# The order of a fused attention and graph-attention kernel laid out anew: five hand-written lists and a table of PSUM banks

## The chip, the cores and the metric

The kernel runs on one core of a Trainium2 chip. The metric is the device time of one execution in microseconds (us); lower is better. Five instruction streams work side by side: TensorE (PE, matrix products, with weight loads shown apart as PEld), ScalarE (ACT), VectorE (DVE), GpSimd (POOL) and SyncE (SP), which here only issues DMAs. They meet through semaphores alone.

## The reference, cut to what matters

Eight batches of 1024 nodes with 128 features pass two layers over the same 1024x1024 adjacency matrix `adj`. Each layer begins with a layer normalisation and a ReLU and ends with a residual sum.

```
h   = relu(layernorm(x))
# layer 0: attention with 4 heads of 32, softmax taken within each of 8 chunks of 128 keys
s   = clip(q @ k.T / sqrt(32), -10, 10);  s = where(adj == 0, -10, s)
ctx = sum over the chunks of softmax(s of the chunk) @ v of the chunk
x   = x + layernorm(ctx @ Wo.T + bo + h) * gamma + beta
h   = relu(layernorm(x))
# layer 1: graph attention over a full row
Wh  = h @ W
e   = leaky_relu(Wh@a1 [i] + Wh@a2 [j], 0.2), -inf where adj has no edge
x   = x + elu(softmax(e) @ Wh)
```

## The kernel before, in words

All constants (masks and transposed weights) are made once at the start; after that every batch `b` goes through the same operations, and the operations of several batches overlap.

Layer 0 of a batch: `stats_x`, `moments_x`, `rstd_x` and `apply_x` normalise a half of 512 nodes; `turn_x` transposes it; `query`, `key` and `value` are its projections. SP copies the projections into head-separated stacks with DMAs (`stack_query`, `stack_key`, four DMAs each). Then come 32 groups of two heads: `scores` (PE) into one of two PSUM slots, `exp` (ACT), `probs` (DVE, which clips and masks), and for every step of two groups `sums` and `context` (PE), `log_sum` and `inverse` (ACT), `gather` (DVE multiplies, POOL adds). `project`, `residual`, `stats_y`, `rstd_y`, `apply_y`, `gamma`, `beta` and `x1` end the layer. `load_residual` is SP's DMA that brings h and x back for this.

Layer 1 of a batch: `rstd_z`, `apply_z`, `turn_hidden`, `wh`, then `peaks` (DVE, eight row maxima with the mask), `row_shift` (POOL), `near_row` and `base_row` (PE), sixteen times `leaky` (DVE), `hide` (mask added, on POOL or DVE) and `gat_exp` (ACT), then `share` (PE, eight of them), `invert`, `below`, `above`, `exp_below`, `add_x1`, `add_below` and `store_out`.

What runs when is written out by hand. There is one table for each engine: `TENSOR`, `SCALAR`, `VECTOR`, `GPSIMD` and `SYNC`. For every batch and name a table gives one place for each index `k`. `in_order(engine)` adds `b * PLACES` (9600) to the place and sorts; each engine then issues its operations in exactly that order, and each operation carries its own semaphore waits. An engine that stands at a wait does nothing of what is listed behind it. A place is only a sort key: a number in it costs nothing by itself.

The string `BANKS` says which of four PSUM banks each operation with a result in `work` uses, in the order of TensorE's list. An operation waits until the user of that bank before it has been read (`free_bank`).

Waits that the prediction touches:

```
dve.wait_ge(x_loaded[k], (b + 1) * 16)                  # stats_x
dve.wait_ge(rest_loaded, 16 * 6)                        # bias_row on DVE
sp.wait_ge(h_stored[k], b * 16)                         # load_x: store_h of the batch before has landed
sp.wait_ge(h_stored[k], (b + 1) * 16)                   # load_residual
act.wait_ge((keys_stacked if before[0] else queries_stacked)[before[1]], (before[2] + 1) * 64)   # query, key
pool.wait_ge(res_loaded[k], 32 * (b + 1))               # residual, beta
act.wait_ge(see_made, 2 * k - 1)                        # cast (ACT)
```

`rest_loaded` counts the six small loads (W, two of a, bo, gamma, beta) that SP issues behind the eight 512 KB loads of `adj`. `parts` holds one half of a projection until its stack DMAs have read it, so `query` and `key` on ACT wait for stacks. `edges` on DVE makes the masks of one row tile; the first `probs` needs four of them.

Of the kernel before, what the change touches and what calls it, by code (L numbers as in the profile page):

```python
# [52 lines left out]
        "weights": [1817, 2924],  # L53
        "value": [1829, 2012],
        "scores": [2254, 2300, 2571, 2745, 2879, 3124, 3420, 3617, 3781, 4002, 4175, 4427, 4560, 4782, 4946, 5197,
            5361, 5526, 5778, 5911, 6075, 6248, 6381, 6633, 6721, 6975, 7314, 7447, 7699, 7778, 8030, 8120],
        "bias_row": [2498],
        "sums": [2957, 3179, 3836, 4230, 4614, 5089, 5252, 5670, 5966, 6524, 6776, 7030, 7502, 7833, 8181, 8659],
        "context": [3267, 3672, 4057, 4318, 4837, 5001, 5416, 5581, 6130, 6436, 6864, 7118, 7590, 7922, 8275, 8822],
        "project": [6293, 10229],  # L60
        "turn_hidden": [11515, 13038],
        "to_row": [11870, 13239],
        "wh": [13845, 14952, 15066],
        "base_row": [17051, 17141],
        "near_row": [17349, 19413],
        "share": [19632, 19850, 20319, 20536, 23047, 23219, 23437, 23773],
    },
    1: {
        "turn_x": [-6225, -4877],
        "query": [-5128, -1171],  # L70
        "key": [-3776, -2374],
        "value": [-2241, -1084],
        "scores": [-1217, -996, -833, -669, -505, -337, -174, -10, 154, 451, 584, 779, 1030, 1171, 1423, 1497,
            1862, 1960, 2224, 2357, 2528, 2704, 3084, 3130, 3392, 3506, 3726, 3830, 4081, 4433, 4479, 4818],
        "sums": [-614, -282, 45, 342, 834, 1226, 1552, 2103, 2412, 2759, 3185, 3884, 4136, 4622, 5036, 5243],
        "context": [-450, -119, 254, 922, 1314, 1640, 1753, 2015, 2596, 2976, 3274, 3973, 4324, 4534, 4873, 5664],
        "project": [2868, 9680],
        "turn_hidden": [8121, 12296],
        "to_row": [12163, 12745],
        "wh": [14729, 14961, 15120],  # L80
        "base_row": [15684, 16561],
# [1702 lines left out]
```

## Time and profile before

| what | value |
|---|---|
| time, median of 3 runs | 720.74 us (719.3 to 720.92) |
| profiled execution, time | 718.64 us |
| profiled execution, span of the trace | 716.9 us |
| DVE busy | 662.4 us (92%) |
| PE busy | 651.6 us (91%) |
| ACT busy | 651.6 us (91%) |
| POOL busy | 526.8 us (73%) |
| DMA | 68.53 MB |

The span is what lies between the first and the last instruction of the trace; the device time of the same execution is 1.7 us longer. The busy share is an average over a start, a long middle and an end that look different.

### The profile page before, as it was taken

The page shows a single profiled execution, that of the slowest core. Times are in us where ns is not written, and L with a number is a line of the kernel's source. Part 1 is how long each engine was busy: PE and PEld are TensorE (multiplying, and loading weights), DVE is VectorE, ACT ScalarE, POOL GpSimd, SP SyncE. Part 2 cuts the span into 40 slices and gives each one's busy share as a digit, 9 for nine tenths or more (in the row PEclk, how much of TensorE's full clock was granted, in tenths as well). Part 3 has the DMA queues.
Part 4 walks back from the last instruction along what each step waited for, and adds up shares of the span by engine and source line. Part 5 has one row for each costly group of instructions (what it writes and reads, how often), then busy time and mean ns, then how long its engine had stood idle before and what let it go on. Part 6 is the DMA issues. An engine that isn't in the chain of part 4 may idle for free.

```text
span 716.9 us, 13598 instructions
## 1 busy us (share of the span) xinstructions
PE 651.6 (91%) x4393; PEld 348.5 (49%) x4393; DVE 662.4 (92%) x1165; ACT 651.6 (91%) x1140; POOL 526.8 (73%) x629
## 2 busy tenths in 40 slices
PE   4389999999899999998999999999999999994976
PEld 2333333344345563546436464557336463564865
DVE  3599999999999999998999999999999999989976
ACT  6399999998999999998999999999999999987655
POOL 2324648656589877978789578998778779998864
PEclk9799999999999999999999999999999999998888
DMA  8742132324121225233222234222222312010111
GB/s 282 236 157 103 60 118 104 103 89 161 63 84 46 93 71 176 75 104 111 80 77 81 90 104 152 91 77 71 83 96 78 114 53 96 23 53 16 51 52 46
DMA packets 58647, 68.53 MB, mean 96 GB/s; under 512 B 5328, under 2 KB 35024, under 8 KB 58576
## 3 DMA queue, kind: packets, MB, share of 16 engines
q1 hardware_dynamic: 57568, 67.39, 27.9%
q8 instruction: 36, 0.59, 0.3%
q10 hardware_dynamic: 1008, 0.26, 0.2%
q14 instruction: 35, 0.29, 0.1%
HBM read 21.50 MB, written 12.58 MB: 48 GB/s over the span
## 4 chain that ended last, share of the span: by engine, by line
PE 39%; ACT 18%; DVE 17%; POOL 10%; issue 10%; DMA 5%; SPq 3%; DVEq 0%; ACTq 0%; POOLq 0%
PE work L1726 11%; PE score L1643 9%; DVE probs L1451 8%; PE work L1660 7%; PE work L1654 6%; ACT score L1296 6%; POOL ring L1248 3%; ACT ring L1364 3%; DVE ring L1542 2%; ACT inverse L1303 2%; ACT inverse L1306 2%; DVE scaled L1477 2%; DVE near_row L1521 2%; SPq L1098 1%; PE work L1618 1%
## 5 line engine op out<-in xcount | busy, mean ns | idle before, releaser
L1451 DVE SCALAR_TENSOR_TENSOR probs<-score,cap 128x1024 f32<-128x1024 f32 x256 | 307.9, 1214 | 11.6 <-ACT score L1296 9.0
L1296 ACT ACTIVATE score<-score 128x1024 f32<-128x1024 f32 x256 | 259.1, 1022 | 6.7 <-PE score L1643 5.2
L1643 PE MATMUL score<-query_stack,key_stack 128*128 128x512 f32 x512 | 188.3, 452 | 14.1 <-DVE probs L1451 10.3
L1223 POOL TENSOR_TENSOR gathered<-gathered,scaled 128x512 f32<-128x512 f32 x112 | 150.3, 1342 | 44.2 <-DVE scaled L1477 41.7
L1248 POOL TENSOR_TENSOR ring<-ring,see_t 128x512 f32<-128x512 f32 x112 | 134.5, 1211 | 22.4 <-DVE ring L1542 21.9
L1643 PEld LDWEIGHTS score<-query_stack,key_stack 128*128 128x128 f32 x512 | 78.6, 189 | 135.8 <-DVE probs L1451 104.7
L1660 PE MATMUL work<-probs,ones 128*32 128x512 f32 x1024 | 135.3, 604 | 1.0 <-DVE scaled L1477 0.4
L1654 PE MATMUL work<-probs,value 128*32 128x512 f32 x1024 | 133.6, 600 | 0.2
L1726 PE MATMUL work<-wh,ring 128*128 128x130 f32 x896 | 110.6, 279 | 12.8 <-ACT ring L1364 11.9
L1726 PEld LDWEIGHTS work<-wh,ring 128*128 128x128 f32 x896 | 107.1, 194 | 23.9 <-issue 16.1
L1364 ACT ACTIVATE ring<-ring,wh 128x512 f32<-128x512 f32 x128 | 90.0, 729 | 9.7 <-POOL ring L1248 7.7
L1306 ACT ACTIVATE inverse<-inverse 128x512 f32<-128x512 f32 x128 | 81.2, 639 | 0.4
L1477 DVE TENSOR_TENSOR scaled<-work,inverse 128x512 f32<-128x512 f32 x112 | 75.7, 680 | 4.8 <-ACT inverse L1306 3.9
L1303 ACT ACTIVATE inverse<-work 128x512 f32<-128x512 f32 x128 | 76.8, 603 | 2.2 <-PE work L1660 1.2
L1542 DVE SCALAR_TENSOR_TENSOR ring<-work,wh,to_row 128x512 f32<-128x512 f32 x96 | 69.6, 739 | 0.0
L1521 DVE CUSTOM_DVE_ANT_0 near_row<-to_row,see 128x1024 f32<-128x1024 f32 x48 | 67.1, 1397 | 0.7 <-ACT to_row L1342 0.3
L1654 PEld LDWEIGHTS work<-probs,value 128*32 128x32 f32 x1024 | 24.9, 108 | 60.9 <-issue 41.3
L1178 POOL TENSOR_TENSOR small<-small,eps 128x4 f32<-128x4 f32 x48 | 14.6, 304 | 54.1 <-DVE small L1430 53.8
L1660 PEld LDWEIGHTS work<-probs,ones 128*32 128x32 f32 x1024 | 24.7, 108 | 57.6 <-issue 43.3
L1181 POOL TENSOR_TENSOR small<-small,minus_half 128x4 f32<-128x4 f32 x48 | 49.6, 1034 | 3.8
L1253 POOL TENSOR_TENSOR gat_out<-gat_out,gat_x 128x256 f32<-128x256 f32 x30 | 25.0, 835 | 12.0 <-ACT gat_out L1382 12.0
L1670 PE MATMUL work<-h_t,w_t 128*128 128x512 f32 x64 | 33.4, 606 | 0.5 <-issue 0.2
(117 smaller groups left out, 844.5 us busy)
## 6 DMA issues: line engine op xcount, KB each, us to landing
query_stack<-parts SPq DMA_DIRECT2D x64, 256.0 KB, 2.6
key_stack<-parts SPq DMA_DIRECT2D x56, 256.0 KB, 2.5
x_in<-in_x SPq DMA_DIRECT2D x16, 256.0 KB, 3.2
h_kept<-x_in SPq DMA_DIRECT2D x16, 256.0 KB, 2.6
res<-h_kept SPq DMA_DIRECT2D x16, 256.0 KB, 2.9
h<-in_x SPq DMA_DIRECT2D x16, 256.0 KB, 3.4
x_kept<-res SPq DMA_DIRECT2D x16, 256.0 KB, 2.2
gat_x<-x_kept SPq DMA_DIRECT2D x32, 128.0 KB, 2.3
```

Of the source, the lines that this page charges most:

```text
L1223: nc.gpsimd.tensor_tensor(sums, sums, scaled[:, k % SCALED], ALU.add).then_inc(gathered_step, 1)
L1248: nc.gpsimd.tensor_tensor(ring[:, k, :], ring[:, k, :], see_t[:, k % CHUNKS, side], ALU.add).then_inc(hidden_done, 1)
L1296: nc.scalar.activation(some, some, ACT.Exp, scale=DH ** -0.5).then_inc(exp_done, 1)
L1303: nc.scalar.activation(inverse[:, k % LOGS], work[:, bank, :], ACT.Ln).then_inc(work_read[bank], 1)
L1306: nc.scalar.activation(inverse[:, k % LOGS], inverse[:, k % LOGS], ACT.Exp, scale=-1.0).then_inc(share_ready, 1)
L1364: nc.scalar.activation(ring[:, k, :], ring[:, k, :], ACT.Exp, bias=ends[:, k % CHUNKS, 3:4]).then_inc(gat_exp_done, 1)
L1451: nc.vector.scalar_tensor_tensor(out=probs[:, group_of(b, k) % KEPT], in0=score[:, h:h + GROUP, :], scalar=LOW, in1=caps.broadcast_to([P, ...
L1477: nc.vector.tensor_tensor(to, work[:, bank, :], inverse[:, k % LOGS], ALU.mult).then_inc(work_read[bank], 1)
L1643: last = nc.tensor.matmul(score[:, head, :], key_stack[:, head, chunk * P:(chunk + 1) * P], query_stack[:, head, half * HALF:(half + 1) * ...
L1654: last = nc.tensor.matmul(work[h * DH:(h + 1) * DH, bank, :], value[:, chunk, h * DH:(h + 1) * DH], of_head(b, k, h), start=True, stop=True)
L1660: last = nc.tensor.matmul(work[h * DH:(h + 1) * DH, bank, :], ones[:, :], of_head(b, k, h), start=True, stop=True)
L1726: last = nc.tensor.matmul(work[:, bank, part * (SIGNS + D):(part + 1) * (SIGNS + D)], ring[:, half * CHUNKS + jt, k % TILES * P:(k % TILES ...
```

## The change

All five lists and `BANKS` are new. The set of listed operations is the same on every engine (763 on PE, 929 on ACT, 795 on DVE, 405 on POOL, 158 on SP), and so are the operations' code, waits and buffers. Which `hide` runs on DVE and which on POOL is unchanged too. What differs is the order: 556 positions of PE's list, 725 of ACT's, 591 of DVE's, 313 of POOL's and 114 of SP's hold another operation. No operation is further from its old position than 24 positions on PE, 55 on ACT, 61 on DVE, 31 on POOL and 10 on SP.

The start of DVE's list, before and after (places in parentheses, /1 is batch 1, the others batch 0):

```
before: stats_x0 (410) moments_x0 stats_x1 moments_x1 (629) cast0 see0 see1 cast1 edges0 stats_x0/1 (1491) see2
        moments_x0/1 see3 key0 (1664) query0 (1730) edges1 see4 edges2 cast2 edges3 see5 edges4 probs0 (2444)
        cast3 probs1 bias_row (2731) probs2 query1 key1 ...
after:  stats_x0 (410) moments_x0 stats_x1 moments_x1 (640) bias_row (1092) see0 cast0 see1 see2 key0 (1384) cast1
        edges0 query0 (1641) see3 edges1 cast2 edges2 edges3 see4 key1 see5 edges4 probs0 (2454) probs1
        stats_x0/1 (2681) query1 probs2 moments_x0/1 ...
```

The start of SP's and ACT's lists:

```
SP before:  store_h0 load_x0/1 load_residual0 store_h1 stack_key0 stack_query0 load_x1/1 load_residual1 ...
SP after:   store_h0 load_residual0 stack_key0 stack_query0 store_h1 load_x0/1 load_x1/1 load_residual1 ...
ACT before: apply_x0 first_weights cast0 apply_x1 mask0 turn_x0 cast1 mask1 key0 query0 mask2 cast2 turn_x1 value0
            mask3 cast3 weights0 mask4 value1 exp0 ...
ACT after:  apply_x0 first_weights cast0 turn_x0 cast1 key0 mask0 mask1 query0 apply_x1 mask2 turn_x1 mask3 cast2
            value0 key1 mask4 value1 exp0 ...
```

Some distances in places between an SP entry and the entry on another engine that waits for its DMAs (all lists hold batch times 9600 plus the place):

| issued by SP | waited for by | before | after |
|---|---|---|---|
| load_residual, half 1, batch 3 | POOL residual | 29416 to 29746, 330 | 29240 to 29831, 591 |
| stack_key, half 1, batch 5 | ACT query, half 1, batch 5 | 38607 to 38970, 363 | 37763 to 38885, 1122 |
| load_residual, half 0, batch 6 | first of POOL residual and beta | 50320 to 50650, 330 | 49820 to 50382, 562 |
| stack_query, half 0, batch 7 | ACT key, half 0, batch 7 | 50400 to 50937, 537 | 49418 to 50456, 1038 |
| load_x1, quarters 0 to 3, batch 6 | POOL add_x1 | 806, 338, 731, 882 | 264, 265, 409, 535 |

The smallest gap between one `share` and the next entry of PE's list is 172 places before and 179 after; between one `rstd` and the next entry of POOL's list 174 and 185. The first `probs` of batch 0 stands at 2444 before and at 2454 after, the last of batch 7 at 60562 and 60263, the last entry of SP's list at 67794 and 67724.

The diff, cut to the tables' beginnings:

```diff
 TENSOR = {
     0: {
-        "turn_x": [893, 1259],
-        "mask": [1104, 1169, 1594, 1751, 1946, 2432, 3466, 3531],
-        "key": [1400, 2100],
-        "query": [1487, 2345],
...
-        "bias_row": [2498],
...
+        "turn_x": [932, 1794],
+        "bias_row": [1049],
+        "mask": [1132, 1284, 1471, 1624, 2111, 2370, 3000, 4176],
+        "key": [1197, 2012],
+        "query": [1350, 2177],
...
 VECTOR = {
     0: {
         "stats_x": [410, 540],
-        "moments_x": [499, 629],
-        "cast": [1080, 1300, 2090, 2557],
-        "see": [1141, 1174, 1568, 1630, 1926, 2280, 7276, 7423],
-        "edges": [1361, 1796, 1960, 2150, 2314, 3110, 3745, 4162],
-        "key": [1664, 2931],
-        "query": [1730, 2865],
...
-        "bias_row": [2731],
...
+        "moments_x": [510, 640],
+        "bias_row": [1092],
+        "see": [1130, 1236, 1326, 1706, 2191, 2290, 4895, 7401],
+        "cast": [1164, 1450, 1870, 3471],
+        "key": [1384, 2225],
+        "edges": [1511, 1740, 1931, 2061, 2324, 3645, 4419, 5396],
+        "query": [1641, 2758],
...
 SYNC = {
     0: {
-        "store_h": [891, 1257],
-        "load_residual": [1171, 2082],
-        "stack_key": [1742, 3132],
-        "stack_query": [1892, 2942],
...
+        "store_h": [920, 1992],
+        "load_residual": [1190, 2365],
+        "stack_key": [1462, 2460],
+        "stack_query": [1727, 2836],
...
     1: {
-        "load_x": [-8469, -7558],
...
+        "load_x": [-7440, -7290],
...
 BANKS = (
-    "0123102120301230032132012012310130210232102101032103010323012101210312310310101201210130130130232021"
...
+    "0123103210301201323012031203201321301310232023021021032010230130202132323212321212012131321231032013"
...
```

## Rows read from the trace of the kernel before

**Rows 1.** Busy time by stretch: us, PE, PEld, DVE, ACT, POOL, clock, DMA share, GB/s
```profile
0.00:60.00 60.00, 35.74 (x209) 19.11 (x209) 39.42 (x90) 40.90 (x66) 17.45 (x38) 0.89 0.62 206
60.00:640.00 580.00, 561.61 (x3780) 279.33 (x3780) 559.58 (x954) 562.23 (x967) 454.67 (x524) 1.00 0.27 91
640.00:717.00 77.00, 54.28 (x416) 50.01 (x404) 63.40 (x123) 48.50 (x110) 54.73 (x70) 0.87 0.14 41
```

**Rows 2.** Timeline of DVE, 0 to 45 us: start, duration, engine, line, operation, idle before
```profile
6.46 0.38 DVE L1430 BATCH_NORM_AGGREGATE small<-small 128x2 f32<-128x6 f32 x4
10.19 0.69 DVE L1583 CAST ring<-probs 128x1024 bf16<-128x1024 int32 x1 [3.36 <-DMA probs<-in_adj]
...
13.80 0.69 DVE L1583 CAST ring<-probs 128x1024 bf16<-128x1024 int32 x1 [2.19 <-DMA probs<-in_adj]
...
24.36 0.87 DVE L1423 BATCH_NORM_STATS2 small<-x_in 128x6 f32<-128x128 f32 x4 [8.58 <-DMA x_in<-in_x]
...
31.40 0.43 DVE L1593 TENSOR_SCALAR ring<-ring 128x1024 bf16<-128x1024 bf16 x1 [0.45 <-ACT ring L1398]
...
36.40 1.23 DVE L1451 SCALAR_TENSOR_TENSOR probs<-score,cap 128x1024 f32<-128x1024 f32 x1 [0.95 <-ACT score L1296]
...
39.27 0.28 DVE L1483 TENSOR_TENSOR rows<-work,rows 128x128 f32<-128x128 f32 x1
...
40.63 0.74 DVE L1459 SCALAR_TENSOR_TENSOR parts<-work,bias_col,parts 128x512 fp32r<-128x512 f32 x1
```

**Rows 3.** Timeline of SP, 0 to 36 us: the DMAs of the start, as issued
```profile
12.01 0.45 SPq L1094 DMA_DIRECT2D rows<-in_L_gnn_beta  x1
12.51 0.44 SPq L1116 DMA_DIRECT2D h_kept<-x_in  x1
21.64 0.38 SPq L1113 DMA_DIRECT2D x_in<-in_x  x1
...
29.46 2.57 SPq L1098 DMA_DIRECT2D query_stack<-parts  x4
```

**Rows 4.** Tile rows until 45 us: issue to landing of its loads
```profile
DMA to landing us min/median/max: 8.3/8.9/8.9
```

**Rows 5.** Chain that ended last, 0 to 45 us: start, length, what
```profile
12.51 9.06 DMA h_kept<-x_in
...
31.42 3.06 DMA query_stack<-parts
```

**Rows 6.** Timeline of POOL around 313 us, and of ACT and PE behind it
```profile
316.52 1.28 POOL L1197 TENSOR_TENSOR res<-res,rows 128x512 f32<-128x512 f32 x1 [3.34 <-DMA h<-in_x]
...
324.53 0.72 ACT L1364 ACTIVATE ring<-ring,wh 128x512 f32<-128x512 f32 x1 [2.53 <-POOL ring L1248]
...
325.40 3.81 PE L1726 MATMUL work<-wh,ring 128*128 128x130 f32 x32 [2.30 <-ACT ring L1364]
```

**Rows 7.** Timeline of ACT around 412 us
```profile
412.42 0.69 ACT L1320 ACTIVATE parts<-work,bias_col 128x512 fp32r<-128x512 f32 x1 [1.58 <-DMA key_stack<-parts]
```

**Rows 8.** Timelines of POOL, ACT and PE around 535 us
```profile
532.25 1.30 POOL L1207 TENSOR_TENSOR h<-h,rows 128x512 f32<-128x512 f32 x1 [2.10 <-DMA h<-in_x]
...
534.87 0.69 ACT L1320 ACTIVATE parts<-work,bias_col 128x512 fp32r<-128x512 f32 x1 [1.40 <-DMA query_stack<-parts]
...
538.63 3.81 PE L1726 MATMUL work<-wh,ring 128*128 128x130 f32 x32 [1.43 <-ACT ring L1364]
```

**Rows 9.** Chain that ended last, 213 to 224 us: one share (16 PE records)
```profile
219.45 1.78 PE work L1726 x16
```

**Rows 10.** DMA issues by line: count, KB each, median us from issue to landing
```profile
h<-in_x SPq DMA_DIRECT2D x16, 256.0 KB, 3.4
...
gat_x<-x_kept SPq DMA_DIRECT2D x32, 128.0 KB, 2.3
```

**Rows 11.** The instructions of L1521 (peaks): count, ns min/median/max, first and last start
```profile
L1521 DVE CUSTOM_DVE_ANT_0 near_row<-to_row,see x48: 1183/1220/2286, 149.3 to 588.1; 128x1024 f32<-128x1024 f32 x48
```

**Rows 12.** Timeline of DVE at the last probs of batch 7
```profile
634.85 1.23 DVE L1451 SCALAR_TENSOR_TENSOR probs<-score,cap 128x1024 f32<-128x1024 f32 x1 [0.16 <-ACT score L1296]
```

More of the change, by code:

```diff
@@ L59 @@
[L59 to L66, printed above, removed]
-    },
-    1: {
[L69 to L81, printed above, removed]
-        "near_row": [15979, 17724],
-        "share": [17815, 18033, 18974, 19192, 20946, 21119, 21721, 22007],
-    },
@@ new lines @@
+        "apply_x": [751, 1613],
+        "first_weights": [906],
+        "cast": [1022, 1217, 2001, 2526],
+        "turn_x": [1117, 1860],
+        "key": [1313, 2144],
+        "mask": [1371, 1463, 1769, 1909, 2203, 2930, 3530, 4293],
+        "query": [1554, 2622],
+        "value": [2096, 2295],
+        "exp": [2343, 2435, 2680, 2772, 3022, 3167, 3414, 3671, 3763, 4007, 4098, 4438, 4530, 4777, 4977, 5172,
+            5317, 5614, 5809, 6003, 6153, 6362, 6609, 6700, 6945, 7090, 7441, 7532, 7745, 7890, 8143, 8235],
@@ new lines @@
+        "load_residual": [1190, 2365],
+        "stack_key": [1462, 2460],
+        "stack_query": [1727, 2836],
+        "store_x1": [7702, 11869],
+        "load_x1": [7952, 8495, 20910, 21006],
+        "store_out": [21527, 22088, 23914, 25394],
+    },
+    1: {
+        "load_x": [-7440, -7290],
+        "store_h": [-6173, -4810],
+        "stack_query": [-4466, 77],
+        "stack_key": [-2473, -1370],
+        "load_residual": [-19, 3195],
+        "store_x1": [5452, 11358],
+        "load_x1": [14120, 15901, 18945, 20556],
+        "store_out": [18893, 20239, 22087, 23468],
+    },
@@ new lines @@
+    2: {
+        "load_x": [-15503, -14122],
+        "store_h": [-13573, -11450],
+        "stack_query": [-7979, -3595],
+        "stack_key": [-6008, -4413],
+        "load_residual": [-1670, 2528],
+        "store_x1": [4568, 9004],
+        "load_x1": [12352, 12754, 16883, 17648],
+        "store_out": [17925, 20063, 20926, 22651],
+    },
+    3: {
+        "load_x": [-20625, -19569],
+        "store_h": [-18799, -18065],
+        "stack_query": [-11092, -5345],
+        "stack_key": [-9216, -6978],
+        "load_residual": [-3251, 440],
+        "store_x1": [2656, 7331],
+        "load_x1": [10607, 11564, 15907, 17554],
+        "store_out": [16185, 18004, 19054, 23837],
+    },
@@ new lines @@
+    6: {
+        "load_x": [-24805, -23115],
+        "store_h": [-18488, -17807],
+        "stack_query": [-16541, -9170],
+        "stack_key": [-14304, -11198],
+        "load_residual": [-7780, -4470],
+        "store_x1": [-2436, 1754],
+        "load_x1": [6494, 6682, 6849, 7196],
+        "store_out": [6955, 7144, 7455, 8172],
+    },
+    7: {
+        "load_x": [-27745, -24983],
+        "store_h": [-22163, -19694],
+        "stack_query": [-17782, -11029],
+        "stack_key": [-16346, -14511],
+        "load_residual": [-10527, -6787],
+        "store_x1": [-5354, -4026],
+        "load_x1": [-2093, -1778, -294, -95],
+        "store_out": [-27, 66, 472, 524],
```

1176 lines of the change are left out of this document (574 added, 602 removed).

## The prediction, on record before the change was run

> **What bounds the kernel now.** I read the busy times by stretch first [rows 1]. In the long middle, 60 to 640 us, PE, DVE and ACT are each busy for 559.6 to 562.2 of 580 us. No single engine is the bound there: three queues run at 97%, and each loses 18 to 20 us to waits. A new order can't remove work; in the middle it can only move those 20 us. The first 60 us are different (DVE 39.4 busy, so 20.6 idle), and so is the end (13.6 of 77 idle on DVE, 28.5 on ACT, 22.7 on PE). All that can be won lies in about 20 us at the start, 20 in the middle and part of 14 at the end.
>
> The timeline of DVE's start shows where the first 20 us go [rows 2]. After its last `moments_x` at 6.84 us DVE waits five times before the first `probs` at 36.40: 3.36 and 2.19 us for loads of `adj`, 8.58 for the first half of x of batch 1, then 0.45 and 0.95. The sum is 15.53, so 29.56 - 15.53 = 14.03 us of that stretch is work. The 8.58 us comes from `stats_x0/1`, which stands ahead of `key0` and `query0`, with the whole stacking of keys and queries behind it. The chain of the start says why its data is late [rows 3, 5]: SP issues `store_h0` at 12.51 behind all the loads, the store takes 9.06 us to land, and only then, at 21.64, does SP issue `load_x0/1`, which DVE gets at 24.36.
>
> In the middle I looked for the waits that reach PE or ACT. Three stand out. At 313 us POOL waits 3.34 us for `load_residual`, is late with `hide`, and ACT then loses 2.53 us and PE 2.30 [rows 6]. At 412 us ACT waits 1.58 for the DMAs of `stack_key` [rows 7]. At 532 to 538 us POOL waits 2.10 for `load_residual` and ACT 1.40 for `stack_query`, and PE then loses 1.43 [rows 8].
>
> **The change part by part.** No operation is added or removed, so the busy times should stay; only gaps move. The sum is made against the profiled execution's own 718.64 us (span 716.9 and 1.7 around it); the median of the runs, 720.74, is 2.1 above it.
>
> *The start.* `stats_x0/1` goes behind `probs1`, so its 8.58 us leave the path. But `bias_row` now stands directly behind `moments_x1`, and it waits for all six small loads. The last of them is issued at 12.01 [rows 3], and the tile's slowest load takes 8.9 us [rows 4]: 20.9 us. Nothing in the new lists changes what SP issues up to there, so this landing stays. DVE is blocked from 6.84 to 20.9, 14.1 us in one piece, where it lost 3.36 + 2.19 + 8.58 = 14.1 in three. ACT's second `cast` (behind `see0`), PE's second `mask` and everything after them stand behind it too. So one stall takes the place of another of the same length. What is left is the order behind it. The work ahead of the first `probs` is 14.03, plus `key1` and `bias_row` (0.74 + 0.28), less `stats_x0/1` and its moments (0.87 + 0.38): 13.8 us. DVE reaches `probs0` at 20.9 + 13.8 = 34.7; with 0.3 for the wait of `see2` for ACT's cast, 35.0. Is it ready for it? ACT's entries from that cast to `exp0` are 1126 places apart, 11.3 us if a place is 10 ns; from 21.5 that is 32.8, the exp takes 1 us: 33.8. The query stack is 549 places behind `bias_row`: 20.9 + 5.5 + 0.74 = 27.1, the last of its four issues 2.0 later, landed after 3.06: 32.2, where it is 34.48 now [rows 3, 5]. Both lie under 35.0. (A place is 10 ns closely enough: from the first to the last `probs` 58118 places took 634.85 - 36.40 = 598.5 us, 10.3 ns each [rows 2, 12].) Against 36.40 that is 1.4 us early, and 0.2 more work is left behind it. I take -1.2 us. Bounds: -3.5, if nothing but DVE's work counted and the stack's 2.3 us came in full; +1.5, if ACT, which now does `apply_x1` and two mask copies after 21.5 us instead of before, is the later one. The value stands nearer the DVE sum because that was worked out entry by entry.
>
> *The three waits in the middle.* The new SP list gives each of those DMAs more room. `load_residual` had 330 places twice and gets 591 and 562; a median load of this kind lands 3.4 us after its own issue, with its partner issued before it [rows 10], so 5.6 us hide it and 3.3 didn't. `stack_key` of batch 5 goes from 363 places to 1122, `stack_query` of batch 7 from 537 to 1038. What these waits cost the path is what PE lost, or ACT where PE lost nothing: 2.30 + 1.58 + 1.43 = 5.3 us. A removed wait is partly given back, since the engine then meets the next one (in the middle all three stay near 97%). I take two thirds, -3.5; bounds 0 and -5.3. Four `load_residual` entries of batches 0 and 1 stand only some 400 places ahead of their user, less than a landing, but POOL is 73% busy and idles there; I cost them at nothing. If POOL were the late engine they would cost 0.5 us each.
>
> *The pace of the lists.* A `share` takes 1.78 us in the chain [rows 9]; the old list leaves it 172 places and the new 179. With 56 of them that is 56 x 0.07 = 4 us by which PE's neighbours on the other lists stood too early. The new order is laid out for the durations that the trace shows, so engines should stand at waits less. The price can't be read from a row; its bounds are 0 and the 18 us of the middle's idle less the 5.3 already counted. I take -1.
>
> *The end.* From the last `probs` to the end the two lists run the same way: 7232 places before, 7461 after, and the trace took 716.9 - 634.9 = 82 us. The last `probs` stands 299 places earlier and the end 70. I cost the end at nothing. `load_x1` of batch 6 loses its room (264 to 535 places instead of 338 to 882) but lands in 2.3 us [rows 10], so it is just hidden; a second transfer in front of it would cost about 1 us each time.
>
> Sum: -1.2 - 3.5 - 1.0 = -5.7 us, 712.9 for the profiled execution and, with 2.1, **715.0** for the median.
>
> **The rivals.**
>
> *The waits come back elsewhere.* With some 2450 positions changed, the middle's 20 us of idle may just be dealt anew: three known waits go and three others come. For it: each engine of three is at 97%, and the old list too had kept most DMAs far enough ahead. Against: the shortest distances of the new SP list are longer. It leaves the start's -1.2: 719.5.
>
> *Contention (slower).* `peaks` usually takes 1.22 us on DVE, but up to 2.29 [rows 11]; on average over the 48 it is 1.40 by the page's group, so 48 x 0.18 = 8.6 us are lost in this order. If the new order lets these operations meet POOL's twice as often, that is +8.6 on an engine that is 97% busy. With the rest of the sum it gives 715.0 + 8.6 = 723.6; it decides once the extra passes 5.7 us. The Trainium skill, GPSIMD Engine Reference, section Specifications, says that the SBUF interfaces are shared with VectorE, with contention for DVE instructions with two SBUF inputs; `peaks` is such a one until batch 5. By that rule the loss depends on what lies beside it, which a reordering changes. Against it: POOL's list has as much work as before, and only the overlap counts.
>
> *The start turns out later.* If ACT's chain behind 21 us sets the first `probs` at 38 us, the start costs +1.5 and the whole gives 717.7.
>
> *The change does more.* If the pacing takes 6 us of the middle's idle instead of 1: 710.
>
> **How the numbers follow.** The forecast 0.47 (its own range 712 to 718, which holds the later start too), back elsewhere 0.22, contention or another lasting new wait 0.13, more 0.18. What a measurement can tell from no change is about 0.3%, 2.2 us: faster means below 718.6, slower above 722.9. Forecast and more are faster (0.65), and of back elsewhere a fifth (0.04); the rest of that is the same (0.18), and 0.03 of the contention case falls there too; 0.10 is slower. The range reaches to the better case at 708.5 and to 721.5, which takes in back elsewhere; about 0.2 is left out.
>
> **What would show it.** In DVE's timeline one wait of 14 us before `bias_row` that ends near 20.9, no wait at `stats_x0/1`, and the first `probs` near 35.0; above 36.4 the step on the start is wrong. No wait of POOL above 1 us for `h` in batches 3 and 6, none above 1 us of ACT for stack DMAs; DVE's idle in 60 to 640 us at 15 us or less instead of 20.4. The mean of `peaks` at 1.40 or below; at 1.5 the contention rival is right. The last `probs` near 629 to 631 us and 82 to 84 us from there to the end; a longer end, with waits for `x_kept` loads or of PE for `ring`, would make the prediction wrong, as would new waits of 2 us and more of PE in the middle.

## The result, and the profile after

| | before | after | ratio, 95% interval |
|---|---|---|---|
| first comparison, medians of 4 and 4 runs | 720.36 us | 708.95 us (708.66 to 709.65) | 0.9845 [0.9828, 0.9862] |
| both run again, medians of 18 and 6 runs | 717.77 us | 709.33 us | 0.9878 [0.9852, 0.9905] |
| span of the first profiled execution | 716.9 us | 706.9 us | |
| span of the second one | 716.9 us | 707.2 us | |

By the ratios the change gains 11.2 us in the first comparison and 8.8 in the second, where 5.7 were forecast. The time lies at the better end of the range. The sign and the places of the gain were forecast; the forecast size was about half of what came.

**The busy times by stretch** of the kernel after, with the columns of [rows 1]:

```profile
0.00:60.00 60.00, 38.69 (x229) 18.50 (x229) 41.97 (x95) 43.24 (x70) 19.53 (x44) 1.00 0.60 206
60.00:640.00 580.00, 563.86 (x3840) 287.90 (x3837) 566.98 (x964) 562.43 (x974) 456.88 (x526) 1.00 0.27 92
640.00:707.00 67.00, 45.19 (x330) 41.85 (x329) 53.29 (x108) 43.72 (x98) 46.62 (x61) 0.88 0.15 44
```

DVE's idle time between 60 and 640 us went from 20.4 to 13.0 us. That was forecast as 15 or less. ACT's hardly moved (17.8 to 17.6) and PE's fell by 2.3. The window holds later work than in the kernel before, so it is a coarse measure; the stretches below are a better one.

**The timeline of DVE's start**, which answers to [rows 2]:

```profile
6.50 0.38 DVE L1431 BATCH_NORM_AGGREGATE small<-small 128x2 f32<-128x6 f32 x4
19.96 0.29 DVE L1484 TENSOR_TENSOR rows<-work,rows 128x128 f32<-128x128 f32 x1 [13.08 <-DMA rows<-in_L_gnn_beta]
...
22.37 0.75 DVE L1460 SCALAR_TENSOR_TENSOR ring<-work,bias_col,ring 128x512 fp32r<-128x512 f32 x1 [0.16 <-ACT ring L1321]
...
34.64 2.34 DVE L1452 SCALAR_TENSOR_TENSOR probs<-score,cap 128x1024 f32<-128x1024 f32 x2
```

There is one wait of 13.08 us, at `bias_row`, in the place of three (3.36, 2.19 and 8.58). It ends at 19.96 and not at 20.9, because the last small load is issued at 12.26 and lands after 7.7 us, not 8.9 as in [rows 4]. Behind it DVE works almost without a gap up to the first `probs` at 34.64. The forecast was 35.0.

**The places of the three waits**, in the timelines of POOL and ACT (they answer to [rows 6], [rows 7] and [rows 8]):

```profile
312.13 1.28 POOL L1198 TENSOR_TENSOR res<-res,rows 128x512 f32<-128x512 f32 x1
...
403.95 0.74 ACT L1321 ACTIVATE parts<-work,bias_col 128x512 fp32r<-128x512 f32 x1
...
525.41 1.29 POOL L1208 TENSOR_TENSOR h<-h,rows 128x512 f32<-128x512 f32 x1
...
524.01 0.69 ACT L1321 ACTIVATE parts<-work,bias_col 128x512 fp32r<-128x512 f32 x1
```

No row has a bracket: POOL no longer waits for h and x of batches 3 and 6, nor ACT for a stack.

**The group of `peaks`** by form, and its line on the page (busy, mean ns, idle before it). They answer to [rows 11]:

```profile
L1522 DVE CUSTOM_DVE_ANT_0 near_row<-to_row,see x48: 1186/1242/2322, 145.4 to 578.9; 128x1024 f32<-128x1024 f32 x48
L1522 DVE CUSTOM_DVE_ANT_0 near_row<-to_row,see 128x1024 f32<-128x1024 f32 x48 | 70.8, 1474 | 1.1 <-DVE peak L1522 0.6
```

The mean rose from 1397 to 1474 ns, so DVE does 48 x 0.077 = 3.7 us more work in these operations. The contention rival had named twice the old loss, +8.6 us, as its case; the rise was less than half of that.

**The last `probs`** of batch 7, which answers to [rows 12]:

```profile
625.32 1.22 DVE L1452 SCALAR_TENSOR_TENSOR probs<-score,cap 128x1024 f32<-128x1024 f32 x1
```

From there to the end it is 706.9 - 625.3 = 81.6 us, where it was 82.1. Three of the prediction's signs were missed: it had the last `probs` at 629 to 631 us, 82 to 84 us behind it, and the mean of `peaks` at 1.40 us or below.

**Where the time came from.** At six points of the lists the same set of operations stands ahead in both orders, on every engine: near places 7700, 15300, 35300, 43400, 52500 and 62200. The time at which DVE ends its last `probs`, `leaky` or `peaks` ahead of each point cuts the span into stretches in which DVE has the same work, to a few instructions; the other engines' work is the same up to what they do early or late at the cuts. Executions with one order in a stretch agree there to a few tenths of a microsecond in most of them, although the times of whole runs scatter by 2. So a change of half a microsecond can be seen in a stretch when it can't in the total. First the kernel before, then the kernel after, with the columns of [rows 1]:

```profile
0.00:91.22 91.22, 66.57 (x401) 30.42 (x401) 69.42 (x141) 71.67 (x116) 36.83 (x61) 0.93 0.49 165
91.22:169.27 78.05, 76.08 (x468) 30.10 (x472) 74.36 (x124) 75.99 (x121) 49.58 (x66) 1.00 0.33 112
169.27:373.99 204.72, 196.62 (x1334) 99.20 (x1326) 199.87 (x343) 198.11 (x342) 163.65 (x190) 1.00 0.28 93
373.99:456.93 82.94, 80.10 (x558) 42.69 (x556) 81.19 (x145) 80.93 (x145) 66.31 (x77) 1.00 0.32 109
456.93:552.31 95.38, 93.25 (x647) 53.13 (x644) 91.02 (x157) 91.67 (x164) 79.76 (x89) 1.00 0.23 78
552.31:650.27 97.96, 95.00 (x674) 52.10 (x672) 92.77 (x156) 89.14 (x160) 84.78 (x91) 1.00 0.20 63
650.27:716.91 66.64, 44.01 (x325) 40.81 (x324) 53.78 (x107) 44.13 (x100) 45.94 (x61) 0.84 0.15 44
```

```profile
0.00:88.13 88.13, 65.74 (x401) 28.92 (x401) 69.39 (x141) 71.02 (x115) 33.40 (x60) 1.00 0.49 171
88.13:165.77 77.64, 75.73 (x470) 29.59 (x472) 74.54 (x125) 75.61 (x120) 50.52 (x67) 1.00 0.33 116
165.77:366.25 200.48, 195.36 (x1332) 100.24 (x1332) 198.79 (x343) 196.00 (x339) 163.92 (x190) 1.00 0.28 94
366.25:448.74 82.49, 79.44 (x548) 43.01 (x544) 80.33 (x147) 80.54 (x145) 67.33 (x80) 1.00 0.28 96
448.74:543.27 94.53, 92.16 (x643) 51.37 (x643) 92.06 (x154) 92.62 (x165) 79.52 (x85) 1.00 0.27 93
543.27:640.89 97.62, 95.00 (x692) 54.17 (x691) 94.72 (x157) 90.66 (x166) 82.61 (x91) 1.00 0.19 60
640.89:706.93 66.04, 44.30 (x322) 40.96 (x321) 52.40 (x107) 42.94 (x96) 45.73 (x61) 0.88 0.15 45
```

The table takes in the executions of this study whose lists have the one or the other order in a stretch and in the one ahead of it, 5 to 10 for each mean (lengths in us, mean and range). Three kernels that would belong there are not in it, and they matter for the scatter: `m_old_stats_late` with 207.9 us and `n_best2` with 201.8 in the stretch to 35300, and `h_mid_new` in the last three stretches, with 66.4 us in the last.

| stretch, in places | old order | new order | gained |
|---|---|---|---|
| start to 7700 | 90.4 (89.4 to 91.2) | 89.3 (88.1 to 90.4) | 1.1 |
| to 15300 | 78.0 (77.9 to 78.1) | 77.7 (77.6 to 77.8) | 0.3 |
| to 35300 | 204.7 (204.1 to 205.9) | 200.5 (200.4 to 200.8) | 4.2 |
| to 43400 | 83.0 (82.9 to 83.0) | 82.5 (82.5 to 82.5) | 0.5 |
| to 52500 | 95.3 (94.8 to 95.6) | 94.5 (94.5 to 94.5) | 0.8 |
| to 62200 | 98.1 (97.9 to 98.6) | 97.6 (97.6 to 97.7) | 0.5 |
| to the end | 67.1 (66.6 to 68.0) | 65.3 (64.3 to 66.2) | 1.7 |

The sum is 9.1 us; the 1.7 of the last row is taken before rounding. Only in the start do the ranges overlap, also with those three. In the last stretch ACT has 96 instructions left where it had 100, and PE 322 where it had 325, so a part of its gain may be work that these engines had done ahead of the cut. Nearly half of the gain lies in one stretch, from place 15300 to 35300, and there DVE's idle time fell from 204.72 - 199.87 = 4.85 to 1.69 us in the pair shown. The wait of POOL at 313 us [rows 6] is in that stretch.

Between 448.74 and 640.89 the two columns of DVE say something else: its idle time fell from 4.36 + 5.19 to 2.47 + 2.90 us, by 4.2, but it was busy 3.0 us longer, and only 1.2 us came out. That is where the slower `peaks` are: the 16 of these stretches that read two SBUF tiles took 22.0 us together before and 25.8 after. How much of the gain they took was not measured by itself.

### The profile page after: what moved, and what is told of

It is laid out like the page before. It is cut to its first block and busy times, and to the rows that moved or that the text cites. A ratio compares the mean times of both kernels' runs of the same rounds, so it can differ in the third digit from the quotient of the medians.

```text
span 706.9 us, 13598 instructions
## 1 busy us (share of the span) xinstructions
PE 647.7 (92%) x4393; PEld 348.3 (49%) x4393; DVE 662.2 (94%) x1165; ACT 649.4 (92%) x1140; POOL 523.0 (74%) x629
## 5 line engine op out<-in xcount | busy, mean ns | idle before, releaser
L1644 PE MATMUL score<-query_stack,key_stack 128*128 128x512 f32 x512 | 186.4, 451 | 18.9 <-DVE probs L1452 17.2
L1224 POOL TENSOR_TENSOR gathered<-gathered,scaled 128x512 f32<-128x512 f32 x112 | 154.4, 1379 | 53.5 <-DVE scaled L1478 52.6
L1727 PEld LDWEIGHTS work<-wh,ring 128*128 128x128 f32 x896 | 107.2, 194 | 17.8 <-issue 7.6
L1307 ACT ACTIVATE inverse<-inverse 128x512 f32<-128x512 f32 x128 | 82.1, 644 | 0.1
L1522 DVE CUSTOM_DVE_ANT_0 near_row<-to_row,see 128x1024 f32<-128x1024 f32 x48 | 70.8, 1474 | 1.1 <-DVE peak L1522 0.6
L1655 PEld LDWEIGHTS work<-probs,value 128*32 128x32 f32 x1024 | 27.2, 109 | 65.4 <-issue 43.6
L1661 PEld LDWEIGHTS work<-probs,ones 128*32 128x32 f32 x1024 | 22.6, 108 | 50.5 <-issue 39.1
L1671 PE MATMUL work<-h_t,w_t 128*128 128x512 f32 x64 | 35.9, 643 | 0.0
L1179 POOL TENSOR_TENSOR small<-small,eps 128x4 f32<-128x4 f32 x48 | 12.0, 249 | 31.4 <-DVE small L1431 31.1
L1254 POOL TENSOR_TENSOR gat_out<-gat_out,gat_x 128x256 f32<-128x256 f32 x30 | 26.7, 892 | 9.6 <-ACT gat_out L1383 9.6
```

The lines of the kernel that those rows point to most:

```text
L1224: nc.gpsimd.tensor_tensor(sums, sums, scaled[:, k % SCALED], ALU.add).then_inc(gathered_step, 1)
L1522: nc.vector.tensor_tensor_reduce(out=near_row[:, :], in0=late_row if b in LATE else to_row[:, :], in1=see[:, k, :], scale=1.0, scalar=-3e3 ...
L1644: last = nc.tensor.matmul(score[:, head, :], key_stack[:, head, chunk * P:(chunk + 1) * P], query_stack[:, head, half * HALF:(half + 1) * ...
L1655: last = nc.tensor.matmul(work[h * DH:(h + 1) * DH, bank, :], value[:, chunk, h * DH:(h + 1) * DH], of_head(b, k, h), start=True, stop=True)
L1661: last = nc.tensor.matmul(work[h * DH:(h + 1) * DH, bank, :], ones[:, :], of_head(b, k, h), start=True, stop=True)
L1727: last = nc.tensor.matmul(work[:, bank, part * (SIGNS + D):(part + 1) * (SIGNS + D)], ring[:, half * CHUNKS + jt, k % TILES * P:(k % TILES ...
```

## The experiments

In the kernels that mix the two orders, and in all that move single entries, operations, waits and buffers are as they were; banks are dealt anew only where a mix or a move needs it. Ratios are to the kernel before. Line numbers in these kernels are 97 lower.

### Mixes of the two orders, to find where the gain lies

**The new lists up to a place, the old ones behind it.**

```diff
-for every engine: old[0:]
+for every engine: new[places < 7700] + old[places >= 7700]        # h_new_to_77
+for every engine: new[places < 15300] + old[places >= 15300]      # h_new_to_153
+for every engine: new[places < 35300] + old[places >= 35300]      # h_new_to_353
```

> The new lists up to place 7700 (about 90 us), the old ones behind it. By then the trace of the new kernel is 3.1 us ahead of the old one. Theory 1, the stretches add up: 3.1 us faster than before (717.3). Theory 2, a head start is given back in the queues behind it: 0 to 1 us faster. Theory 3, my prediction's sum for the start: 1.2 us faster.

> The new lists up to place 15300 (about 168 us), the old ones behind. The new kernel's trace is 3.5 us ahead there. Theory 1: 3.5 us faster than before (716.9). Theory 2: 0 to 1 us faster. In both it is no more than 0.5 us from the kernel cut at 7700.

> The new lists up to place 35300 (about 370 us), the old ones behind. The new kernel's trace is 7.7 us ahead there; the stretch holds the wait of 3.34 us for load_residual of batch 3. Theory 1: 7.7 us faster than before (712.7), 4.2 more than with the cut at 15300. Theory 2: 3 us or less.

| new up to place | ratio | median |
|---|---|---|
| 7700 | 0.998 [0.9961, 0.9999] | 718.38 us |
| 15300 | 0.9982 [0.9965, 0.9999] | 718.94 us |
| 35300 | 0.9933 [0.9908, 0.9959] | 715.44 us |

The start alone is worth 1.4 us [0.1, 2.8], and adding the next stretch changes nothing that can be told. With the stretch up to 35300 the gain is 4.8 us. The trace of that kernel was 5.3 us ahead at the join and gave 1.6 back in the stretch behind it (84.56 us instead of 82.9); at the join DVE waits 1.71 us for ACT. So a mix of orders can price what it changes too low.

**The other way round, and the one stretch alone.**

```diff
+old[places < 7700] + new[places >= 7700]                                     # h_old_to_77
+old[places < 35300] + new[places >= 35300]                                   # h_old_to_353
+old[places < 15300] + new[15300 <= places < 35300] + old[places >= 35300]    # h_mid_new
+old[places < 15300] + new[15300 <= places < 23000] + old[the rest]           # h_153_232
```

> The mirror: the old lists up to place 7700, the new ones behind. Theory 1: what the start gives is missing, 11.4 - 3.1 = 8.3 us faster than before (712.1). Theory 2: the later stretches make up for the late start, 10 to 11 us faster (710).

> The old lists up to place 35300, the new ones behind it. By the traces the stretches behind 35300 won 10.0 - 7.7 = 2.2 us. Theory 1, the stretches add up: 2.2 us faster than before. Theory 2, by the times of the kernel with the new lists up to 35300 (4.5 us faster): the remaining 6 to 7 us are behind it, 6 us faster.

> The old lists with only the stretch from place 15300 to 35300 new. Theory 1: 4.2 us faster at place 35300, of which the join gives 1.6 us back as in the kernel with the new lists up to 35300: 2.6 us faster. Without such a loss 4.2. If the start's and this stretch's gains were one thing: 0.

> The old lists with only the stretch from place 15300 to about 23000 new. Both traces say that little is won there (old 78.9, new 77.7 us). If the 4.1 us of the stretch to 35300 are won at the wait near 313 us and behind: 1.2 us at the most here, and the wait of 3.3 us of POOL for load_residual of batch 3 is still there. If a better order ahead of it removes it: that wait is gone and 3 to 4 us are won.

| kernel | ratio | median | gained |
|---|---|---|---|
| old start, all else new | 0.9883 [0.986, 0.9907] | 711.63 us | 8.4 us |
| new from 35300 on | 0.9941 [0.9923, 0.9959] | 713.95 us | 4.2 us |
| new from 15300 to 35300 | 0.9962 [0.9945, 0.9979] | 714.88 us | 2.7 us |
| new from 15300 to 23000 | 1.0011 [0.9991, 1.0032] | 718.28 us | none |

The gain comes from many places and nearly adds up: up to place 35300 and from there on it is 4.8 + 4.2 = 9.0 us. The start is the small part. The new stretch in the middle won 3.9 us in the trace (200.8 us long) and lost 1.6 again at the join, as before. The first part of that stretch alone won 1.0 us and lost it again, and it kept POOL's wait:

```profile
316.02 1.27 POOL L1100 TENSOR_TENSOR res<-res,rows 128x512 f32<-128x512 f32 x1 [3.03 <-DMA h<-in_x]
```

So what the stretch gains lies at that wait or behind it.

### The three waits by themselves

**Taken out of the old lists.** Each waiting entry is moved behind the entries that stood behind it, so that its DMAs have time to land.

```diff
 POOL: gather11/3
-residual1/3
 hide14/1 gather12/3 gather13/3
+residual1/3
 POOL: hide5/4
-beta0/6
 hide6/4 hide7/4
+beta0/6
 ACT:  query1/5 from behind exp6/5 to behind exp7/5;  key0/7 from behind exp23/6 to behind gat_exp5/4
 DVE:  query1/5 to behind peaks4/3;  key0/7 to behind leaky8/4
```

> The old kernel with four entries moved back a little: POOL's residual (half 1, batch 3) behind two hides and two gathers, POOL's beta (half 0, batch 6) behind two hides, ACT's and DVE's query (half 1, batch 5) and key (half 0, batch 7) two to three entries later. The three waits for DMAs of the prediction go without anything else. My prediction: 3.5 us faster (bounds 0 and 5.3). Rival: such a wait is made up for within the next batch, 0 to 1 us.

Measured: 0.9944 [0.9928, 0.9961], 716.45 us against 720.11, a gain of 4.0 us [2.8, 5.2]. ACT's waits for the stacks are gone from the trace. Against the means of the table its trace shows less: 1.2 us in the stretch of the first wait, -0.1 and -0.2 in the two stretches of the other waits, and 1.0 in the next; in all 2. Around the first wait the trace won 2.8 us, but some 40 us ahead of it 1.4 were lost, where ACT waits for another stack:

```profile
273.60 0.69 ACT L1223 ACTIVATE parts<-work,bias_col 128x512 fp32r<-128x512 f32 x1 [1.30 <-DMA query_stack<-parts]
```

The lists there are those of the kernel before, which has no wait at this entry in either of its executions. So a stack that has just enough room in one execution can be late in another, and one trace can miss a microsecond by it. The three waits together are worth about what was forecast in the old lists, and in the trace the first holds most of it.

**Put back into the new lists.** Here one entry moves ahead in POOL's list, towards its load, by three entries and by five.

```diff
 POOL: gather10/3
+residual1/3            # n_new_residual_early2
 gather11/3 add_x1 1/1
+residual1/3            # n_new_residual_early
 gather12/3 hide15/1 add_below1/1
-residual1/3
```

> The new kernel with one entry moved: POOL's residual (half 1, batch 3) three entries forward, ahead of gather12, hide15 and add_below, 255 places behind its load instead of 591. It puts the old wait of some 3 us back and changes nothing else. Theory 1, this one wait is what the stretch to place 35300 won: 3 to 4 us slower than the new kernel. Prediction's rate: 2.3 x 2/3 = 1.5 us slower. Theory 2, the wait is made up for behind it: 0 to 0.5 us.

> The new kernel with POOL's residual (half 1, batch 3) moved forward by five entries, ahead of gather11 too, so that its wait is not 1.3 us as in the first try but 2.5 to 3.5 us. If POOL's lateness reaches ACT and PE as in the old kernel: the stretch 15300 to 35300 takes 203 to 204 us instead of 200.5. If the loss was bound to the old order around it: 201.5 or less.

By three entries POOL waits 1.30 us, and the time is 709.85 us, 0.988 [0.9856, 0.9904]; the stretch is 0.9 us longer (201.38 against 200.5), two thirds of the wait. By five entries POOL waits 3.47 us, as it did in the kernel before, and the time is 713.39 us, 0.9938 [0.9914, 0.9961]: 4.1 us more than the kernel after on the same chip. The stretch to place 35300 of that trace:

```profile
165.91:370.25 204.34, 195.85 (x1332) 100.23 (x1332) 199.07 (x342) 196.01 (x339) 163.56 (x190) 1.00 0.28 92
```

It is 204.34 us long instead of 200.5, 3.8 us more for a wait of 3.47 on an engine that is idle for a quarter of the time. The timelines of POOL, ACT, DVE and PE of that kernel show the way it takes:

```profile
310.54 1.28 POOL L1100 TENSOR_TENSOR res<-res,rows 128x512 f32<-128x512 f32 x1 [3.47 <-DMA h<-in_x]
...
326.79 1.65 ACT L1187 ACTIVATE res<-res,small 128x128 f32<-128x128 f32 x4 [4.35 <-POOL small L1087]
...
329.53 0.75 DVE L1362 SCALAR_TENSOR_TENSOR parts<-work,bias_col,parts 128x512 fp32r<-128x512 f32 x1 [2.82 <-ACT parts L1223]
...
331.91 0.70 PE L1546 MATMUL score<-query_stack,key_stack 128*128 128x512 f32 x2 [1.53 <-DVE probs L1354]
...
337.00 0.74 PE L1546 MATMUL score<-query_stack,key_stack 128*128 128x512 f32 x2 [1.66 <-DVE probs L1354]
```

POOL is late with everything behind that entry. It meets ACT 16 us later, at `apply_y`, which needs `rstd_y` of POOL, and ACT stands for 4.35 us; DVE then stands 2.82 for ACT. PE shows two waits, of 1.53 and 1.66 us, 21 and 26 us behind POOL's. Who reads the cost off PE's first wait behind it, as the prediction did, finds less than half of it.

### The start

**One of the two stalls taken out of the old lists.**

```diff
 DVE: ... edges0
-stats_x0/1
 see2
-moments_x0/1
 see3 key0 ... probs0 cast3 probs1
+stats_x0/1
 bias_row probs2
+moments_x0/1
```

> The old kernel with only stats_x and moments_x of batch 1 on DVE moved behind probs1 and probs2. If the stall at stats_x0/1 holds the start: the 8.58 us wait goes, but SP still stands at load_x until 21.6 us, so the stacks start at 23.5 instead of 26.8 us: 3 us faster. If DVE's work alone counts (it can now use the time before 24.4 us for masks): 5 to 8 us faster. If the start is hidden anyway: 0.

Measured: 1.0048 [1.0028, 1.0068], 723.83 us, slower by 3.5, which none of the theories had. DVE makes its masks early and then meets another wait in the same place. In the timelines of DVE and ACT:

```profile
35.16 1.23 DVE L1354 SCALAR_TENSOR_TENSOR probs<-score,cap 128x1024 f32<-128x1024 f32 x1 [7.87 <-ACT score L1199]
...
34.04 1.93 ACT L1199 ACTIVATE score<-score 128x1024 f32<-128x1024 f32 x2 [7.66 <-PE score L1546]
...
42.95 1.65 ACT L1187 ACTIVATE x_in<-x_in,small 128x128 f32<-128x128 f32 x4 [2.38 <-POOL small L1087]
```

PE waits for the stacks, and SP can't issue them: its own list stands at `load_x0/1` until 21.69 us, where the chain of [rows 5] has it too. The first `probs` is only 1.2 us earlier. Then x of batch 1 is normalised later: ACT stands 2.38 us at `apply_x0/1`, and the fifth `probs` is 3.6 us later than in the kernel before (47.92 against 44.35). Place 7700 is reached at 94.5 us, 4.1 behind the mean. The stretch to 35300 takes 207.9 us, 3.1 more than the mean, though its lists are the old ones: there ACT waits 0.81 us for a stack at 277 us, and POOL waits 3.74 for `load_residual` of batch 3. So in the kernel before two stalls lay over one another, one of DVE and one of SP, and the new lists change both: they put one at `bias_row` on DVE, and `load_residual0` in the place of `load_x0/1` on SP.

**Both stalls taken out of the old lists.**

```diff
 DVE: as above
 SP:  store_h0
+stack_key0 stack_query0
 load_x0/1 load_residual0 store_h1
-stack_key0 stack_query0
```

> As m_old_stats_late, and on SP stack_key0 and stack_query0 issued ahead of load_x0/1, load_residual0 and store_h1. Neither engine then stands behind the store that lands at 21.6 us. If both stalls set the start: first probs near 27 us instead of 36.4, 6 to 9 us faster. If the landings behind the 4 MB of adj hold the stacks too: 3 to 4 us faster.

Measured: 0.9946 [0.9926, 0.9965], 716.3 us, faster by 3.9. The first `probs` is at 28.93 us, 7.5 us earlier; 3.4 us of it are left at place 7700 (87.0 us).

**Both stalls taken out of the new lists.**

```diff
 PE:  turn_x0
-bias_row
 ... mask5
+bias_row
 DVE: moments_x1
-bias_row
 see0 ... probs0 probs1
+bias_row
 stats_x0/1 ...
 SP:  store_h0
-load_residual0
 stack_key0 stack_query0
+load_residual0
 store_h1 load_x0/1 ...
```

> The new kernel with bias_row moved behind probs1 on DVE and behind mask5 on PE, and load_residual0 behind stack_query0 on SP. Its wait of 13.1 us before bias_row goes. If that wait sets the start: first probs near 27 to 29 us instead of 34.6, 5 to 8 us faster than the new kernel (701 to 704). If the start is set by the landings of adj and stacks: 1 to 2 us faster than the new kernel. If bias_row's wait costs nothing since the masks would wait too: 709.

Measured: 0.9757 [0.9722, 0.9791], 702.22 us. Run again it gave 0.9776 [0.9748, 0.9804], 703.56 us against 719.1:

> m_new_no_stall once more, on this chip and in more rounds, as the comparison for n_best2. First measurement: ratio 0.9757. By its trace (13.3 us less span, of which up to 1.5 us may be the start's scatter): 0.979 to 0.983.

The second ratio is a little better than expected. Both times it is the fastest kernel of the study: 16 to 18 us under the kernel before, and by the medians 5 to 7 under the kernel after. Place 7700 is reached at 85.1 and 84.0 us, 4.7 before the mean of the new order, and the stretches behind it are those of the new order. DVE's timeline of the second:

```profile
6.45 0.38 DVE L1333 BATCH_NORM_AGGREGATE small<-small 128x2 f32<-128x6 f32 x4
10.84 0.43 DVE L1489 TENSOR_SCALAR see<-ring 128x1024 bf16<-128x1024 bf16 x1 [4.01 <-ACT ring L1297]
...
24.99 0.75 DVE L1362 SCALAR_TENSOR_TENSOR ring<-work,bias_col,ring 128x512 fp32r<-128x512 f32 x1 [2.24 <-ACT ring L1223]
...
29.26 2.36 DVE L1354 SCALAR_TENSOR_TENSOR probs<-score,cap 128x1024 f32<-128x1024 f32 x2 [1.92 <-ACT score L1199]
```

The wait of 13.08 us has become one of 4.01, the stacks are issued at 15.15 and 17.99 us instead of 23.15 and 25.89, and the first `probs` is at 29.3. SP's timeline in the kernel after shows the second stall that this edit takes away:

```profile
12.73 0.43 SPq L1117 DMA_DIRECT2D h_kept<-x_in  x1
20.64 0.33 SPq L1131 DMA_DIRECT2D res<-h_kept  x1
```

SP issues `store_h0` at 12.73 us and stands at `load_residual0` until 20.64, with the stacks behind it. So the stall at `bias_row`, which the prediction took as given, and the one on SP beneath it cost the new lists 5 to 7 us together. What one of them costs alone was not tried.

**The stacks still earlier.** In both kernels the loads of adj tiles 6 and 7 are issued behind the stacks, and the stacks move to the front of SP's list.

```diff
 on top of the edit above
 SP:
-adj loads 0 to 7 | store_h0 stack_key0 stack_query0 load_residual0 store_h1 load_x0/1
+adj loads 0 to 5 | stack_key0 stack_query0 store_h0 | adj loads 6, 7 | load_residual0 store_h1 load_x0/1   # n_best
+adj loads 0 to 5 | stack_key0 store_h0 stack_query0 load_x0/1 | adj loads 6, 7 | ...                         # n_best2
```

> The version with no stall at the start (m_new_no_stall), with store_h0 issued behind the stacks, and the loads of the last two tiles of adj issued behind them as well, so 1.25 MB less stand ahead of the stacks in the queue. There ACT waited 2.86 us for key_stack and PE 4.30 us for query_stack. If their landing holds the start: first probs at 26 to 27 us instead of 29.9, 2 to 3 us faster than m_new_no_stall. If DVE's mask work holds it: 0 to 1 us.

> As n_best, but SP issues store_h0 between the two stacks and load_x0/1 right behind the second, and only then the last two tiles of adj. In n_best the first probs was at 25.2 us, and 9 of the 11 us were lost again by place 7700: DVE waited 6.45 us for x of batch 1, and ACT 7.8 us. If that late load is all: place 7700 is reached 8 to 10 us ahead of the old kernel, 3 us faster than m_new_no_stall. If the order behind the start is bound to its own pace: no faster than m_new_no_stall.

Measured: 0.9847 [0.9819, 0.9874], 706.96 us, and 0.9827 [0.9799, 0.9855], 706.76 us. Both miss: they bring the first `probs` to 25.2 and 26.4 us and are still slower than the version above. The timelines of DVE, POOL and ACT of the second one show what comes next:

```profile
35.10 0.87 DVE L1329 BATCH_NORM_STATS2 small<-x_in 128x6 f32<-128x128 f32 x4 [2.19 <-DMA x_in<-in_x]
...
37.60 1.28 POOL L1113 TENSOR_TENSOR h<-h,rows 128x512 f32<-128x512 f32 x1 [4.39 <-DMA h<-in_x]
...
41.16 1.65 ACT L1190 ACTIVATE x_in<-x_in,small 128x128 f32<-128x128 f32 x4 [6.35 <-POOL small L1090]
...
43.84 1.22 DVE L1357 SCALAR_TENSOR_TENSOR probs<-score,cap 128x1024 f32<-128x1024 f32 x1 [4.15 <-ACT score L1202]
```

The lists stand at the loads that come due next. In `n_best` that is half 0 of x of batch 1: DVE waits 6.45 us for it. In `n_best2` this half was there in time, and the stall moved on. SP issues the second `load_x` and `load_residual1` only when `store_h1` has landed, from 32.30 us on. DVE waits 2.19 us for the first of them; POOL stands 4.39 us for `load_residual1`, with `rstd_x0/1` listed behind it; `apply_x0/1` on ACT waits for that and holds the `exp` behind it. The first `probs` is 8 to 9 us earlier than in the kernel after, but place 7700 is reached at 87.4 and 87.7 us, 1.9 and 1.6 earlier than its mean; the version above is 5 us earlier at the first `probs` and still 4.7 at that place.

### Both kernels again

> The kernel before, unchanged, profiled a second time, to see how far one trace repeats. Theory: behind place 7700 the stretches agree within 0.3 us, the start differs by up to 1.5 us with the landing of the loads. Rival: the stretches scatter by 1 us and more, then the reading by stretches is worth little.

> The new kernel, unchanged, timed beside the kernel before in more rounds and profiled a second time. Adding up the stretches over all traces so far (start 1.0, then 0.3, 4.1, 0.5, 0.7, 0.3 and 0.7 us) gives 7.6 us, 1.05%; the first measurement gave 1.55%, 11.2 us. If the stretches tell it: ratio near 0.9885. If the first measurement: 0.9845. My prediction was 0.992.

Both comparisons stand in the first table, and both executions in the table of stretches. The second ratio, 0.9878, is near what the stretches had said, 0.9885. Of the kernel before, the stretches behind place 7700 repeat to 0.1 us in three cases and to 0.3 in the last; the one to 52500 is 0.5 us shorter and the one with POOL's wait 1.2 us longer (205.9), so the theory holds for most of them and the rival for that one. The kernel before has POOL's wait again, at nearly the same time and length:

```profile
314.83 1.28 POOL L1197 TENSOR_TENSOR res<-res,rows 128x512 f32<-128x512 f32 x1 [3.04 <-DMA h<-in_x]
```

## Why the prediction was right in kind and wrong in size

| step of the prediction | forecast | measured | by what |
|---|---|---|---|
| the start | -1.2 | -1.1 by stretches, -1.4 [-2.8, -0.1] timed | first stretch; new lists to 7700 |
| first wait, 2.30 x 2/3 | -1.5 | -3.8 by its stretch, -4.1 timed | a wait of 3.47 put back |
| the other two, 3.01 x 2/3 | -2.0 | at most -1.3 | their stretches, 0.5 and 0.8 |
| pace of the lists | -1.0 | about -1.2 | 4.2 - 3.8, 0.3 and 0.5 |
| the end | 0 | -1.7 | last stretch |
| sum | -5.7 | -9.1 by stretches | |

*The start* was right nearly step by step. DVE's three waits became one at `bias_row`, of 13.1 us where 14.1 was forecast. The landing was 0.9 us sooner than its bound, the work behind it 0.6 longer than the sum, and the first `probs` came at 34.6 and 34.8 us against 35.0. That the later start would turn out worse was wrong. What the prediction didn't ask is what the new stall itself costs; moving it behind `probs1`, and `load_residual0` behind the stacks, gave the best version. The first profiled execution after had a granted clock of 1.00 in the first 60 us and the one before 0.89 [rows 1]; what that is worth in the start was not measured.

*The three waits* went as forecast. **The step that failed** is the price: "What these waits cost the path is what PE lost". It sized the first wait at 2.30 us by PE's idle time right behind it and then took two thirds. Put back alone into the new lists, a wait of 3.47 us cost 3.8 in its stretch, all of it, where 1.5 for one of 3.34 was forecast; one of 1.30 cost 0.9. Between 15300 and 35300 three engines run at 96 to 99%, so POOL's lateness finds no slack to vanish in once it arrives. PE's idle time right behind it is not a measure of it: the loss shows up in later waits, 4.35 us on ACT, 2.82 on DVE and twice 1.5 to 1.7 on PE. The claim of a partial return was right for the other two: their stretches gained 1.3 us where 2.0 were taken for the waits alone, and with the waits undone in the old lists these stretches gained nothing and the next one 1.0. The three waits come to 3.8 + 1.3 = 5.1 us at most instead of 3.5; undone together in the old lists they gave 4.0 [2.8, 5.2], and the forecast of 3.5 lies within that. So that the price was too low is shown in the new lists alone, and how the first wait and the pace of its stretch share the 4.2 us was measured only there.

*The pace* was sized at 1, with bounds of 0 and 12.7. Beside the waits it gave about 1.2 us, in small amounts. No single entry was found for it, and the effect of the bank table alone was not tried. The prediction's "some 2450 positions changed" is 2299 by the list of the change; none of its terms hangs on it.

*The end* was costed at nothing, since the tail from the last `probs` runs the same way. In the first pair of executions it nearly did (81.6 against 82.1), and the last stretch, which begins 15 us later, shrank by 0.6. Over all executions that stretch shrank by 1.7, with ranges that don't meet, and the time from the last `probs` to the end fell from 82.4 to 80.9 us in the mean (81.8 to 83.5 with the old order, 79.9 to 81.8 with the new). That is the second term that was mis-sized; what in the new order of the end does it was not taken apart.

*The rivals.* That the waits come back elsewhere is refuted for the whole, and is what happened in the kernels with a join, where 1.6 us came back. The work in `peaks` grew by 3.7 us, at a mean of 1474 ns, under the 1.5 us that the prediction named as the sign of contention and above the 1.40 it expected; the rise lies between 448 and 641 us. The Trainium skill, GPSIMD Engine Reference, section Specifications, says that VectorE instructions with two SBUF inputs contend with GpSimd. The traces agree: in both kernels every `peaks` above 1.5 us has both inputs in SBUF and POOL at work beside it, those without POOL beside them took 1.21 to 1.23 us, and the 16 that read `score` in PSUM took 1.21 to 1.23 us too, 14 of them with POOL at work. No run here changed the overlap by itself. "The change does more" at 710 was the nearest case, for another reason than its own: not the pacing gave the largest part, but one wait.

*What stays open.* The stretches give 9.1 us, the two comparisons 11.2 and 8.8, whose intervals barely overlap. The start's scatter is 1 us either way between executions, which covers some of it. The three waits undone gave 4.0 us timed and 2 in the one trace, of which the stack that came late at 273 us explains 1.4. What in the new order shortens the end, and the 1.2 us of pace, have a place but no cause.

## What to carry to other kernels

A wait on an engine with a quarter of its time idle can cost the program its full length, when the engines that read from it are full (3.8 us for 3.47 here, and 0.9 for 1.30): price it by taking it out of the list, or putting it back, and not by what the bound engine shows right behind it. Cut two traces at points where the same work stands ahead in both, and compare the stretches; that shows half microseconds that the total hides. Where a start has a stall, look for a second one under it before moving either, and then for the input that comes due next: a first result 5 us earlier was worth 4.7 us, and one 9 us earlier only 1.9, since the loads due next had not moved with it.

## What the runs showed of the hardware

In the new order the stretches of 78 to 98 us in the middle repeated to 0.2 us over six executions and more, and the one of 200 us to 0.4 in all but one, `n_best2` with 201.8, while the first 90 us varied from 88.1 to 90.4 us with the same lists. In the old order the stretch of 205 us, in which POOL waits for its load, took from 204.1 to 207.9 us. The start holds the landings of the 4 MB of adj: the small loads behind them took 7.7 us in one kernel and 8.3 to 8.9 in the other [rows 4], though they are issued at the same time to within 0.3 us. `peaks`, the same instruction on the same shape, took from 1.18 to 2.32 us, and 18 of 64 took more than 1.5 us after the change where 13 had before, all of them with two SBUF inputs and POOL at work beside them. The clock granted to TensorE over the first 60 us was 0.89 of full speed before [rows 1] and 1.00 after, and 0.91 and 0.97 in the second executions. The start was 3.1 us shorter in the first pair and 0.7 in the second.
